# Key-major scores in the first attention: maxima taken off by three contraction rows, no transposes there, no trips through DRAM

## What is computed

```python
def bitnet_linear(x, weight, scale):       # first attention's projections
    s = maximum(mean(abs(weight), axis=1), 1e-08)
    return nan_to_num(einsum('bsi,oi->bso', x, sign(weight / s[:, None])) * (s * scale))

q, k, v = (bitnet_linear(x, w, c) for w, c in ...)        # 32, 8, 8 heads of 16
attn = softmax(q @ k.T / sqrt(16))                         # 256 queries x 256 keys
x = layernorm(x + bitnet_linear(attn @ v, o_weight, o_scale))
attn = softmax(x_heads @ ctx_heads.T / sqrt(16) + mask)    # 256 queries x 512 keys
x = layernorm(x + attn @ ctx_heads)
x = layernorm(x + x @ W.T + bias)                          # W from bit planes and a table of 16
```

## Time and profile before

| | us |
|---|---|
| median of 3 runs | 343.99 |
| lowest, highest | 343.56, 347.1 |
| span of the profiled execution | 348.7 |
| PE busy | 296.6 (85%) |
| DVE busy | 283.0 (81%) |
| POOL busy | 188.2 (54%) |
| ACT busy | 159.3 (46%) |

### The profile page before, as it was taken

One profiled execution on the slowest core, in us unless ns is written; L12 is line 12 of the kernel. 1 busy time (PEld: TensorE's weight loads), 2 busy tenths in 40 slices (PEclk: granted clock), 3 DMA queues, 4 the chain that ended last, 5 costly groups with the idle time before them and its releaser, 6 DMA issues.

```text
span 348.7 us, 6649 instructions
## 1 busy us (share of the span) xinstructions
PE 296.6 (85%) x2216; PEld 187.2 (54%) x2216; DVE 283.0 (81%) x937; ACT 159.3 (46%) x285; POOL 188.2 (54%) x276
## 2 busy tenths in 40 slices
PE   8989649787999977787999879999997899999880
PEld 8679316454665544344555445556644466556830
DVE  2869688999696799996958999999999986573746
ACT  2211305555564354443734546676764566247010
POOL 2153089999595345884725557777774665320000
PEclk9989858999899998998999989999999999999997
DMA  7907793399970002591000013970000000000001
GB/s 238 368 24 154 147 120 140 91 102 96 199 89 2 1 2 68 103 96 7 4 1 2 1 51 74 99 51 2 2 1 3 0 2 2 0 33 30 2 0 60
DMA packets 37427, 21.51 MB, mean 62 GB/s; under 512 B 21008, under 2 KB 33040, under 8 KB 37392
## 3 DMA queue, kind: packets, MB, share of 16 engines
q1 hardware_dynamic: 36432, 20.62, 35.1%
q10 hardware_dynamic: 960, 0.46, 0.5%
HBM read 15.70 MB, written 5.37 MB: 60 GB/s over the span
## 4 chain that ended last, share of the span: by engine, by line
PE 51%; DVE 31%; issue 10%; DMA 5%; SPq 1%; DVEq 1%; ACT 1%; ACTq 0%
PE PT L980 19%; PE PO L996 11%; PE PA L956 6%; DVE SM L750 4%; PE PS L1045 4%; PE PA L959 3%; DVE SM L745 3%; DMA SM<-in_wq_T 3%; PE PM L1022 3%; PE PS L1051 2%; DVE stats L776 2%; PE PS L1055 2%; DVE root L789 1%; DVE SM L606 1%; PE PA L1051 1%
## 5 line engine op out<-in xcount | busy, mean ns | idle before, releaser
L478 POOL TENSOR_SCALAR SM<-SM,mx 128x256 f32<-128x256 f32 (+1 forms) x256 | 171.9, 685 | 99.3 <-DVE mx L745 64.3
L529 ACT ACTIVATE PTs<-PT 128x512 f32<-128x512 f32 x192 | 113.3, 597 | 110.7 <-PE PT L980 110.4
L980 PE MATMUL PT<-ident,SM 128*128 128x128 f32 x768 | 121.4, 284 | 0.0
L980 PEld LDWEIGHTS PT<-ident,SM 128*128 128x128 f32 x768 | 93.6, 145 | 29.6 <-ACT PTs L529 19.5
L745 DVE CUSTOM_DVE_ANT_0 SM<-PA,maskq 128x512 f32<-128x512 f32 x128 | 85.0, 686 | 20.8 <-PE PA L956 20.0
L996 PE MATMUL PO<-PTs,V 128*32 128x256 f32 x768 | 62.4, 397 | 0.2 <-ACT PTs L529 0.2
L956 PE MATMUL PA<-KA,QA 96*128 96x512 bf16 x128 | 49.4, 389 | 14.7 <-DVE mx L745 11.8
L750 DVE TENSOR_SCALAR_CACHE_REDUCE SM<-PA 128x256 f32<-128x256 f32 x128 | 47.0, 415 | 12.5 <-PE PA L959 9.8
L959 PE MATMUL PA<-KA,QA 96*128 96x256 bf16 x128 | 27.5, 302 | 15.5 <-DVE SM L750 12.4
L996 PEld LDWEIGHTS PO<-PTs,V 128*32 128x32 f32 x768 | 15.1, 108 | 26.2 <-ACT PTs L529 16.0
L956 PEld LDWEIGHTS PA<-KA,QA 96*128 96x128 bf16 x128 | 12.6, 99 | 21.8 <-DVE mx L745 13.8
(11 more groups left out here) (141 smaller groups left out, 309.6 us busy)
## 6 DMA issues: line engine op xcount, KB each, us to landing
QA<-dq SPq DMA_DIRECT2D x24, 96.0 KB, 6.6
QA<-dq SPq DMA_DIRECT2D x6, 256.0 KB, 10.8
KA<-dk SPq DMA_DIRECT2D x6, 256.0 KB, 19.8
dq<-parts SPq DMA_DIRECT2D x4, 384.0 KB, 3.4
xT<-in_x_T SPq DMA_DIRECT2D x1, 1024.0 KB, 7.5
SM<-in_wq_T SPq DMA_DIRECT2D x1, 1024.0 KB, 10.8
SM<-in_wo_T SPq DMA_DIRECT2D x1, 1024.0 KB, 14.6
x<-in_x_tok SPq DMA_DIRECT2D x1, 1024.0 KB, 21.6
```

Of the source, the lines that this page charges most:

```text
L478: nc.gpsimd.tensor_scalar(row, row, -1.0, mx[:, u % SM_RING, n:n + 1], ALU.mult, ALU.add).then_inc(sub_done, 1)
L529: nc.scalar.activation(PTs[:, c % PT_RING, j * 512:(j + 1) * 512], PT[:, (2 * c + j) % T_RING, :], ACT.Exp, scale=-1.0).then_inc(exp_done, 1)
L980: last = nc.tensor.transpose(PT[:, n % T_RING, (i % 4) * P:(i % 4 + 1) * P], SM[:, u % SM_RING, i, k * P:(k + 1) * P], ident[:])
```

## The change

- **Scores twice in the first attention.** The query-major scores stay, but VectorE only takes their maxima (`tensor_reduce`, two row blocks in one instruction); nothing is copied to SBUF, nothing subtracted by GpSimd, nothing transposed. The scores that go to exp are made anew by `direct`: keys stationary, two heads' queries moving, straight into the PT bank that exp reads.
- **The maximum as three contraction rows.** KA1 gets three rows of -1, QA three rows with the maximum in three bf16 parts. GpSimd splits the maxima (`split_maxima`, four operations on 128 x 8), TensorE turns them (`turn_maxima`), ScalarE unloads 12 rows (`rows`), and GpSimd issues a DMA that puts them into QA (`send_maxima`). This goes two units ahead.
- **Scores three units ahead** in the first attention, still two in the second: unit 13 makes none.
- **No DRAM trips.** The weights' rows are ordered so that a part's partition is (feature, head); SyncE copies SBUF to SBUF. The queries of x1 go once for both tiles of a sequence.
- **Moved.** The reduction of the output weights goes to unit 1, its matmuls to unit 2, the output scales to unit 3. GpSimd's context split, V2 and output weights go in pieces between units. Values are projected into PO, not PA. Layernorm 1 writes into O in (feature, head) order and GpSimd copies it back to x (`keep_x1`).

```diff
+def upcoming(u):
+    if u + SCORES_AHEAD < L1:
+        return [(u + SCORES_AHEAD, i) for i in range(fills(u + SCORES_AHEAD))]
+    if L1 <= u + 2 < UNITS:
+        return [(u + 2, i) for i in range(fills(u + 2))]
+    return []
...
+            def send_k(ka, source, ready):
+                for s in range(SLOTS):
+                    dma_tile(sp, ka[s * HD:(s + 1) * HD, :, :], source[:, K_PART[s]], ready)
+            def send_q(n):
                 b, o0, o1 = Q_SENDS[n]
                 sp.wait_ge(q_split, 2 + n)
-                if (o0, o1) == (0, DT):
-                    dma_tile(sp, dq1[b].rearrange("s (o p) n -> p (s o) n", p=P), q_parts[b].rearrange("p s o n -> p (s o) n"), dq_written)
-                else:
-                    for o in range(o0, o1):
-                        dma_tile(sp, dq1[b, :, o * P:(o + 1) * P].rearrange("s p n -> p s n"), q_parts[b][:, :, o], dq_written)
-            def read_q(n):
-                b, o0, o1 = Q_SENDS[n]
-                feats, heads, toks = slice(o0 * P, o1 * P), slice(o0 * P // HD, o1 * P // HD), slice(b * S, (b + 1) * S)
-                sp.wait_ge(dq_written, Q_WRITES[n])
                 for s in range(SLOTS):
-                    dma_tile(sp, QA[s * HD:(s + 1) * HD, heads, toks],
-                             dq1[b, Q_PART[s], feats].rearrange("(h d) n -> d h n", d=HD), qa_ready)
-            write_q(0)
-            sp.wait_ge(dk_written, 16)
-            for s in range(SLOTS):
-                dma_tile(sp, KA1[s * HD:(s + 1) * HD, :, :], dk1[K_PART[s]].rearrange("(g d) n -> d g n", d=HD), ka1_ready)
-            read_q(0)
-            for n in range(1, Q_FIRST):
-                write_q(n)
-                read_q(n)
+                    dma_tile(sp, QA[s * HD:(s + 1) * HD, b, :, o0:o1, :], q_parts[b][:, Q_PART[s], o0:o1, :], qa_ready[n])
+            sp.wait_ge(q_split, 1)
+            send_k(KA1, k_parts, ka1_ready)
+            for n in range(len(Q_SENDS)):
+                send_q(n)
+            sp.wait_ge(qa_ready[-1], 16 * SLOTS)
+            dma_tile(sp, x[:], x_tok.rearrange("(t p) d -> p t d", p=P), ld_xn)
...
+                sp.wait_ge(x1_split, QT * (b + 1))
+                sp.wait_ge(a_full, first_fill(G * (b + 1)))
+                sp.wait_ge(t_full, 2 * first_chunk(G * (b + 1)))
+                rows_of_x1(b, 0, EARLY * R * HD // P, qa2_first[b])
+                rows_of_x1(b, EARLY * R * HD // P, DT, qa2_rest[b])
...
+            def split_maxima(u):
+                pool.wait_ge(sm_ready, first_fill(u + 1))
+                if u >= 2:
+                    pool.wait_ge(rows_full, u - 1)
+                split_ = [mxb[:, u % 2, :, s * R:(s + 1) * R].rearrange("p q r -> p r q") for s in range(MX_PARTS)]
+                whole = mx[:, u % MX_RING, :].rearrange("p (r q) -> p r q", q=QT)
+                left = mx_left[:].rearrange("p (r q) -> p r q", q=QT)
+                link(nc.gpsimd.tensor_copy(split_[0], whole))
+                link(nc.gpsimd.tensor_tensor(left, whole, split_[0], ALU.subtract))
+                link(nc.gpsimd.tensor_copy(split_[1], left))
+                nc.gpsimd.tensor_tensor(split_[2], left, split_[1], ALU.subtract).then_inc(mx_split, 1)
+            def send_maxima(u):
+                pool.wait_ge(rows_out, u + 1)
+                b, g = batch(u), group(u)
+                dma_tile(pool, QA[KR:KRM, b, head_rows(g), g * R // HT, :], mx_rows[:, u % 2, :], rows_in[u % 2])
...
+            between = split_context()
+            for u in range(L1):
+                split_maxima(u)
+                send_maxima(u)
+                if u >= 1:
+                    next(between, None)
...
+            def rows(u):
+                act.wait_ge(rows_full, u + 1)
+                if u >= 2:
+                    act.wait_ge(rows_in[u % 2], 16 * (u // 2))
+                nc.scalar.activation(mx_rows[:, u % 2, :], PO[0:MX_ROWS, S:2 * S], ACT.Copy).then_inc(rows_out, 1)
...
-                    for q in range(QT):
-                        vec.tensor_scalar(SM[:, u % SM_RING, QT * i + q, 0:S], PA[:, f % 2, q * S:(q + 1) * S], 1.0, None,
-                                          ALU.mult, ALU.max, accum_out=mx[:, u % SM_RING, QT * i + q:QT * i + q + 1]).then_inc(sm_ready, 1)
-                        tick()
+                    vec.tensor_reduce(mx[:, u % MX_RING, QT * i:QT * (i + 1)], PA[:, f % 2, :].rearrange("p (q k) -> p q k", q=QT),
+                                      AX.X, ALU.max).then_inc(sm_ready, 1)
+                    tick()
+                    tick()
...
+            def turn_maxima(u):
+                pe.wait_ge(mx_split, u + 1)
+                if u == 0:
+                    pe.wait_ge(v_out, NT)
+                    pe.wait_ge(const_ready, 4)
+                else:
+                    pe.wait_ge(rows_out, u)
+                for q in range(QT):
+                    last = mm(PO[:, S + q * P:S + (q + 1) * P], mxb[:, u % 2, q, :], identb, start=True, stop=True)
+                last.then_inc(rows_full, 1)
...
+            def direct(u, k, j):
...
+                b, g = batch(u), group(u)
+                if k == 0 and j == 0:
+                    pe.wait_ge(rows_in[u % 2], 16 * (u // 2 + 1))
+                mm(PT[:, n % T_RING, :], KA1[0:KRM, g, b * S + k * P:b * S + (k + 1) * P],
+                   QA[0:KRM, b, g * R % HT + 2 * j:g * R % HT + 2 * j + 2, g * R // HT, :], start=True, stop=True).then_inc(t_full, 1)
...
+                        if layer(u):
+                            turn(u, k, j)
+                        else:
+                            direct(u, k, j)
+                        for v, i in due[j * len(due) // 2:(j + 1) * len(due) // 2]:
+                            scores(v, i)
                     if k >= 1:
                         product(u, k - 1)
                     elif u >= 1:
                         product(u - 1, key_tiles(u - 1) - 1)
+                    if k == 0 and u + ROWS_AHEAD < L1:
+                        turn_maxima(u + ROWS_AHEAD)
+                    if u == 2 and k == 0:
+                        pe.wait_ge(q_out, 1 + B * DT)
+                        sums(PS[:], abs_o, D, 3).then_inc(sums_ready, 1)
...
-                if k == 0 and u == 0:
-                    pe.wait_ge(scales, 4)
                 if k == 0 and u >= 1:
                     pe.wait_ge(po_free, u)
+                if k == 0 and u < L1:
+                    pe.wait_ge(rows_out, min(u + ROWS_AHEAD + 1, L1))
...
+                if u == 1:
+                    dve.wait_ge(ld_wo, 16)
+                    vec.tensor_reduce(abs_o, wo_raw.rearrange("p i (a o) -> p a o i", o=S), AX.X, ALU.add,
+                                      apply_absolute_value=True).then_inc(abs_ready, 1)
+                if u == 3:
+                    output_scales()
```

More of the change, by code:

```diff
@@ L50 @@
 KR = SLOTS * HD
+MX_PARTS = 3
+KRM = KR + MX_PARTS
+MX_ROWS = MX_PARTS * R
+HT = P // HD
 EPS = 1e-5
@@ L64 @@
 SM_RING = 3
+MX_RING = 4
+L1 = B * G
+X1_KEPT = {L1 + 9: 2, L1 + 10: 3}
+ROWS_AHEAD = 2
+SCORES_AHEAD = 3
 PT_RING = 3
@@ L470, in shift @@
             def shift(u):
-                keys = key_tiles(u) * P
                 for i in range(R * QT):
-                    pool.wait_ge(sm_ready, R * QT * u + i + 1)
-                    n = row_block(u, i) if layer(u) else i
-                    row = SM[:, u % SM_RING, n, 0:keys]
-                    nc.gpsimd.tensor_scalar(row, row, -1.0, mx[:, u % SM_RING, n:n + 1], ALU.mult, ALU.add).then_inc(sub_done, 1)
-            for u in range(UNITS):
-                shift(u)
-                if u == 0:
-                    pool.wait_ge(signs, 3)
-                    pool.wait_ge(scales, 4)
-                    for i in range(DT):
-                        nc.gpsimd.tensor_tensor(woT[:, i, :], woT[:, i, :], so, ALU.mult).then_inc(wo_scaled, 1)
+                    pool.wait_ge(sm_ready, first_fill(u) + i + 1)
@@ new lines, in shift, with keep_x1 @@
+                    n = row_block(u, i)
+                    row = SM[:, u % SM_RING, n, :]
+                    nc.gpsimd.tensor_scalar(row, row, -1.0, mx[:, u % MX_RING, n:n + 1], ALU.mult, ALU.add).then_inc(sub_done, 1)
+            between = split_context()
[4 more added lines that the diff above has]
+                    next(between, None)
+            for _ in between:
+                pass
+            def keep_x1(t):
+                pool.wait_ge(x1_ready, t + 1)
+                nc.gpsimd.tensor_copy(x[:, t].rearrange("p (o h d) -> p o h d", o=DT, d=HD), by_dim(O[:, t])).then_inc(x1_kept, 1)
@@ L490, in _ @@
+            for t in range(QT):
+                keep_x1(t)
+            for u in range(L1, UNITS):
+                shift(u)
+                if u in X1_KEPT:
+                    keep_x1(X1_KEPT[u])
         @block.scalar
@@ L563, in _ @@
             fills_left = iter(FILLS_LOW)
+            for u in range(ROWS_AHEAD):
+                rows(u)
             for u in range(UNITS):
@@ L1061, in _ @@
                 scores(1, i)
+            turn_maxima(0)
```

(12 more changed lines are left out.)

219 lines of the change are left out of this document (112 added, 107 removed).

## The result

The changed kernel takes 352.01 us (median of 4 runs, 350.25 to 354.88), the kernel before 344.23 us beside it (4 runs, 343.56 to 347.1). The ratio is 1.0177, 95% interval 1.0125 to 1.0229: **slower by 1.8%**, where 1.6% faster was forecast. Medians are over all runs, while the ratios leave out runs over 1.5% above the fastest of their kernel and are not the quotient of two medians, which would be 1.0226 here. The profiled execution of the changed kernel has a span of 350.3 us, that of the kernel before 348.7. A timed execution is 1.8 to 2.6 us longer than its span, so the one that was profiled for before is longer than all its timed ones. The two traces differ by 1.6 us, the times by 6.1 (by the ratio) to 7.8 (by the medians), so some 5 us of the difference can't be read from the traces.

What follows compares the result with a forecast made beforehand. VectorE was taken to bound the first attention. The terms -1.4 - 4.5 + 0.5 - 3.0 - 1.15 + 0.8 + 3.9 - 0.7 = -5.55 us, off the median 343.99, gave 338.4 us; range 335 to 341, with most rivals 330 to 347.

Steps and rivals of the forecast that it cites:

- -4.5: Maxima on VectorE in the first attention: four reductions at 0.61 us replace eight tensor_scalar per unit, -4.5 us over 16 units.
- -3.0: First attention: with GpSimd quieter, VectorE's table steps and copies get shorter, -3.0 us in all, between 0 and -5.
- the chain of the maxima: Split, turn, unload and DMA of each unit's maxima: 4.35 us a cycle, priced 0; as the bound, a rival, 353 us, chance 0.13.
- Just hidden: 0: In the chain of the maxima: rows land 3.2 us after issue, needed after some 6, and VectorE has other work; cost 0.
- a rival: TensorE's 2.90 us stop and VectorE's 2.7 us without a releaser may go, projection stops shrink: 332 us, chance 0.18.
- The start: Before the first maximum: no DRAM trips bring it 4.85 us earlier, the 3.7 us reduction now stands between maxima; -1.15 in all.
- The boundary: Start of the second attention: sending both tiles' queries in one go costs +3.9 us, the second tile's wait goes, -0.7.
- The clock rival: TensorE stands more and its clock drops, each drop costing a unit some 1 to 2 us; three more make 342; chance 0.07.
- +0.8: At the start: exp is late because the first direct scores need unit 0's maxima split, turned, unloaded and carried by DMA; +0.8 us.
- -7.0: VectorE's terms in the first attention taken together: -4.5 for the maxima, +0.5 for layernorm ticks standing together, -3.0 for quieter GpSimd.
- -1.4: TensorE's removed work counts only in two chunks with an output projection ahead of the scores, 0.7 us each: -1.4 us.

Runs made afterwards that it cites:

- the first experiment: The changed kernel with its bulk loads (x, second attention's keys, mask) issued in twelve pieces of 256 KB from chunk 8 on: 346.25 us, ratio 1.0046 to the kernel before.

## Why the prediction was wrong

**What held.** VectorE bounds the first attention, and its own work shrank as forecast. The changed kernel's VectorE in units 3 and 4:

```profile
77.24 1.27 DVE L816 TENSOR_REDUCE mx<-PA 128x2 f32<-128x512 f32 x2
78.44 0.72 DVE L785 COPY_PREDICATED wqT<-masks,lut 128x512 f32<-128x512 uint8 x1
79.05 1.27 DVE L816 TENSOR_REDUCE mx<-PA 128x2 f32<-128x512 f32 x2
80.37 0.21 DVE L830 RECIPROCAL rsum<-PM 128x8 f32<-128x8 f32 x1
...
84.83 0.21 DVE L830 RECIPROCAL rsum<-PM 128x8 f32<-128x8 f32 x1
```

Two reductions take 1.20 us from start to start (0.60 each, forecast 0.61), the table step 0.72 (0.73), the units 4.26 and 4.46 us (4.2 to 4.3) instead of 4.72 and 4.74. So -4.5 and -3.0 were of the right kind where nothing else stood in the way. Over units 6 to 12 the gain was 2.7 us, 0.4 a unit. Nor did the chain of the maxima become the bound: GpSimd issues in 0.59 us, less than the 1.0 taken, and the longest wait of TensorE for the split is 0.9.

**The step that failed** is in *The chain of the maxima*: "The rows are needed 1.5 units after the issue, some 6 us, and land after 3.2, which hides the landing". The need was as forecast, 5.6 us. The 3.2 is a median over twelve other copies; the maxima's rows of unit 6 landed after 11.5, with the 3 MB under way that SyncE issued in the 7 us around them. Put down as "Just hidden: 0", it cost 4.5 us by the first experiment. Trace and diff had all that was needed: the DMA share of 0.87 in the earlier trace rows, and an order in which three loads follow each other with no wait in between.

The 2.90 us stop of the earlier trace rows, named in a rival as something that may go, did go, and the 6.04 us one came. It belonged to the same heap by the program's order: 64 of L959's matmuls, eight units of eight, stand ahead of it, so the score behind it is the first to read the second sequence's queries. Their six copies were issued from 69.02 and took 10.8 us in the median. The profile names no releaser, so this is read and not shown.

**The start** was better than forecast in time and wrong in place. The first maximum came at 36.33, 6.7 us earlier than before, where 4.85 was forecast. But the forecast took -4.85 and +3.7 as one bargain, -1.15, and didn't ask where the reduction could stand for nothing: VectorE stood 5.04 us ahead of the first maximum, and moving the reduction back there won 3.9. Two more long pieces on VectorE between the maxima weren't priced: the eight instructions that unpack the bit masks take 4.3 us (3.16 before) and TensorE then stands 2.81, and the output scales take 2.8 and TensorE stands 2.29, at a time when only three units of scores lie ahead.

**The boundary**: the split to first score took 5.7 us, forecast 5.6, and the second attention's first maximum came 2.2 us later than before while the rest stood level. The forecast was +3.9 (its own terms, 5.6 less 1.8, give 3.8) and -0.7. GpSimd's copies of x1, which had been set to 0, stretch the table step beside them to 3.05 us; but VectorE stands 2.29 for scores behind it, so in this kernel they cost nothing that shows. What was missing is what follows the stop of 4.7 us on TensorE: the maxima of units 16 and 17 are made at half clock, 1.1 us over before's for the first. Up to unit 14 the boundary cost 4.9, but up to unit 15 only 1.6 to 2.5, so it was not priced too low as a whole.

**The clock rival** had the right price (1 to 2 us a unit, measured 1.5). Its reading of the trace was not right: 2.90 us is not the longest stop, TensorE stood 4.24 us before 50.90. Whether 0.07 was too small a chance stays open, since how much of the loss is the clock alone is not shown. That the clock fell is: 0.74 instead of 0.87 from 43 to 104 us, and 0.56 instead of 1.00 from 140 to 160. A change that takes a tenth of TensorE's work in the first attention away and leaves its stops in place makes the stops a larger share.

**The sum.** Against the forecast of -5.55 stands +6.1 (1.77% of 344), a gap of 11.6 us. The collision is 4.5 of it. Another 2.3 was missing before it: for the start and the first five units the forecast comes to about -2.5 (-1.15, +0.8 and five sixteenths of -7.0), and the table above has -0.2 at unit 4; 1.1 of that are the masks. Units 6 to 12 gained 2.7 us, where seven sixteenths of -7.0 and the -1.4 make 4.5. The rest can't be placed, because the two traces differ by 1.6 us only.

## What to carry to other kernels

When a change adds a small transfer that an engine waits for, list what all queues issue back to back around it, and price it by a landing behind all those bytes and not by a median of other copies. Cutting the bulk into pieces tied to the consumer's progress took the stop away here, and cost the kernel before nothing that shows (0.9969). A long instruction on the engine that bounds belongs into its longest stop, even when what it feeds is needed much later. A change that only thins out the work of an engine should be priced with the clock that its remaining stops bring.

## What the runs showed of the hardware

- A DMA of 12 rows of 512 bytes, issued on another engine's queue, landed after 11.3 to 11.5 us with 3 MB of copies under way, after 5.9 to 6.4 beside 1.5 MB, and after 1.7 to 3.2 away from them. Issued by ScalarE instead of GpSimd beside the 3 MB, it was used 11.6 us after its issue as well. The Trainium skill (DMA: Bandwidth & Descriptors, section Queues, rings and completion order) states that each DMA engine takes turns between its queue rows, a packet at a time. By that alone a small transfer would pass quickly; it didn't, and what held it up is not shown.
- VectorE's predicated copy took 0.72 us by itself, 2.03 beside one strided GpSimd copy and 3.05 beside two. A cast took 1.23 instead of 0.43 beside one.
- A float32 matmul of 128 columns takes 0.228 us, in two entries 0.114 apart.
- With TensorE kept at work through its stop, the granted clock from 140 to 160 us was 0.99 to 1.00 instead of 0.56, and the unit that followed took 7.3 us instead of 8.8.
- The mean granted clock differs by some 0.025 between executions of one kernel. In three kernels with four executions each the span goes with it, by some 3.7 us; in the 39 of the kernel before only loosely.
